# Moving 104 tiles of counting from layer 2 to layer 1 of a four-layer graph network, and placing the turned products later

## What is computed

```python
h = relu(layernorm(x)); x = x + concat(h, mean_over_edges(h[src])) @ W.T + b          # layer 0
h = relu(layernorm(x)); theta = h[dst] - h[src]                                        # layer 1
w = sigmoid(relu(theta @ W1 + b1) @ W2 + b2)
x = x + segment_sum(w * theta, dst) + indegree * (h @ W4 + b4)
h = relu(layernorm(x)); x = x + (h + l2norm(elu(mean(relu(h@Wp.T+bp)[src]) @ Wl.T + bl + h@Wr.T)))  # layer 2
h = relu(layernorm(x)); x = x + segment_sum((h @ Wrel[type])[src] * norm, dst) + h @ Wloop          # layer 3
```

## Time and profile before

| | us |
|---|---|
| median of 3 runs | 6365.12 (6364.78 to 6367.93) |
| the profiled execution, its span from first to last instruction | 6426.8 |
| layer 0, edges | 107.8 to 1240 |
| layer 1, edges | 1304.2 to 3660 |
| layer 2, edges | 3696 to 4315 |
| layer 3, edges | 4526 to 6426.8 |

### The profile page before, as it was taken

One profiled execution on the slowest core, in us unless ns is written; L12 is line 12 of the kernel. 1 busy time (PEld: TensorE's weight loads), 2 busy tenths in 40 slices (PEclk: granted clock), 3 DMA queues, 4 the chain that ended last, 5 costly groups with the idle time before them and its releaser, 6 DMA issues.

```text
span 6426.8 us, 68888 instructions
## 1 busy us (share of the span) xinstructions
PE 3872.2 (60%) x20122; PEld 2959.4 (46%) x20154; DVE 2933.5 (46%) x9989; ACT 1413.8 (22%) x5474; POOL 3972.3 (62%) x4198
## 2 busy tenths in 40 slices
PE   4676766655555565555555578876565565665433
PEld 3333434445544454455455456653344444444332
DVE  7555544556555565556555633342333222222222
ACT  4222122333333333333333401121000000000000
POOL 4556666456666666666666466646566666666665
PEclk7778778777777777777777789998777777777666
DMA  3333333345455454544545455555211111111121
GB/s 107 96 101 110 111 105 116 107 140 155 143 150 148 147 150 144 154 145 141 159 144 151 123 184 198 195 181 178 69 46 46 45 47 45 46 45 46 46 61 46
DMA packets 323521, 734.49 MB, mean 114 GB/s; under 512 B 77056, under 2 KB 164124, under 8 KB 310860
## 3 DMA queue, kind: packets, MB, share of 16 engines
q0 software_dynamic: 172432, 405.32, 23.2%
q1 hardware_dynamic: 148700, 323.81, 14.9%
q10 hardware_dynamic: 2016, 0.92, 0.1%
HBM read 598.71 MB, written 131.05 MB: 114 GB/s over the span
## 4 chain that ended last, share of the span: by engine, by line
another core or an unknown queue 30%; PE 27%; DVE 19%; issue 15%; ACT 4%; DMA 2%; DVEq 1%; SPq 1%; ACTq 0%
PE ps L2574 8%; DVE oneh L1863 6%; PE ps L2559 3%; PE ps L2530 3%; PE ps L2537 2%; DVE ps L1998 2%; PE ps L2469 2%; PE ps L2597 2%; DMA third<-dst_flat 2%; ACT turned_words L1681 1%; DVE third L1990 1%; PE ps L2419 1%; DVE turned_words L1955 1%; DVE tmp L1954 1%
## 5 line engine op out<-in xcount | busy, mean ns | idle before, releaser
L1470 POOL DMA_INDIRECT rows<-tab_rel,third x1299 | 1247.0, 960 | 646.9 <-issue 367.1
L1470 POOL DMA_INDIRECT rows<-tab_h,idx_src x1086 | 1046.7, 964 | 723.4 <-issue 345.8
L1470 POOL DMA_INDIRECT rows<-tab_hp,idx_src x1120 | 1077.1, 962 | 622.5 <-issue 298.8
L2597 PE MATMUL ps<-third 128*128 128x128 f32 x3126 | 607.1, 353 | 501.6 <-issue 295.8
L2530 PE MATMUL ps<-oneh,rows 128*128 128x128 f32 x2598 | 489.1, 340 | 607.1 <-DVE oneh L1863 330.7
L2597 PEld LDWEIGHTS ps<-third 128*128 128x128 f32 x3126 | 539.6, 258 | 593.7 <-issue 355.3
L2574 PE MATMUL ps<-third,h 128*120 128x384 bf16 (+17 forms) x3773 | 715.0, 337 | 65.8 <-issue 34.6
L2530 PEld LDWEIGHTS ps<-oneh,rows 128*128 128x128 f32 x2598 | 432.6, 245 | 695.8 <-DVE oneh L1863 362.6
L1681 ACT ACTIVATE turned_words<-turned_words 128x128 f32<-128x128 f32 x1563 | 463.1, 300 | 690.8 <-DVE turned_words L2003 527.5
L2574 PEld LDWEIGHTS ps<-third,h 128*120 128x120 bf16 (+10 forms) x3773 | 487.8, 133 | 239.4 <-issue 61.3
L1470 POOL DMA_INDIRECT third<-tab_hp,idx_src x443 | 425.9, 961 | 231.7 <-issue 118.5
(11 more groups left out here) (279 smaller groups left out, 5495.4 us busy)
## 6 DMA issues: line engine op xcount, KB each, us to landing
third<-dst_flat SPq DMA_DIRECT2D x390, 256.0 KB
h<-cnt_d SPq DMA_DIRECT2D x48, 1568.0 KB
cnt_d<-h SPq DMA_DIRECT2D x29, 1568.0 KB
cnt_d<-third SPq DMA_DIRECT2D x19, 1568.0 KB
tab_rel<-third SPq DMA_DIRECT2D x49, 512.0 KB
rows<-tab_rel,third POOLq DMA_INDIRECT x1299
rows<-tab_hp,idx_src POOLq DMA_INDIRECT x1120
rows<-tab_h,idx_src POOLq DMA_INDIRECT x1086
```

The lines of the kernel that those rows point to most:

```text
L1470: pool.indirect_dma_start(out=to[:, t, 0:n], out_offset=None, in_=table[:, :], in_offset=bass.IndirectOffsetOnAxis(ap=idx[:, col:col + 1], ...
L2597: last = pe.matmul(ps_t[sl][:, t * P:(t + 1) * P], onehT[:, sl, t * P:(t + 1) * P], pwin[:, st["v"] % 2, :], start=True, stop=True)
```

## The change

The share of layer 0 goes from 880/1563 to 980/1563. Rounded to bundles, it counts 976 tiles where it counted 872, which is six bundles more (of 18, 18, 18, 18, 16 and 16 tiles), and gathers 587 tiles where it gathered 691, 26 groups fewer. Layer 1 makes 192 late counts where it made 296, and stores 13 bundles where it stored 19. In layer 0 alone, `pack_turn` stands five tiles behind `pack_out` where it stood one, and `pack_add` three behind `pack_turn` where it stood one. Layers 2 and 3 keep their work.

```diff
-FIRST_SHARE = 880 / 1563
+FIRST_SHARE = 980 / 1563
+LATE_TURN, LATE_ADD = 5, 3
@@ multiply(u)
                 plan.append(("pack_out", st))
-                yield 0.0
+                for _ in range(LATE_TURN if layer == 0 else 1):
+                    yield 0.0
                 st["added"] = n_added.get(u - 1, 0)
                 plan.append(("pack_turn", st))
-                yield 0.0
+                for _ in range(LATE_ADD if layer == 0 else 1):
+                    yield 0.0
                 plan.append(("pack_add", dict(u=u, sums=sums, turn=n_turn[u], add=s_add.value)))
```

## The result

The changed kernel takes 6287.20 us (median of 4 runs, 6283.21 to 6294.15), the kernel before 6366.52 on the same chip (6364.78 to 6371.44). The ratio is 0.9879, with a 95% interval of 0.9862 to 0.9896: 79 us less, where 65 more were forecast.

A forecast was written before the change was run, and what follows sets the result against it. It took PE to bound layer 0, with gathers as unused cover. Terms +165 - 42 - 25 - 30 = +68 us on the 6365.12 us median gave 6433, said as 6430; range 6400 to 6475, 8 in 10 within 6360 to 6490.

The forecast's parts named there:

- the one on the gathers: Layer 0: gathers run ahead while POOL waits for PE, so fewer of them are worth nothing.
- Six bundles, +165: Layer 0: six added bundles at 27.5 us each, priced from PE's work, cost 165 us (138 to 180).
- 26 groups, -42: Layer 0: 26 fewer groups at 1.6 us each, mainly PE's scatters and turned sums, save 42 us (35 to 57).
- The later turn, -25: Layer 0: counts fill half of the 1.4 us hole before each of 35 turns, saving 25 us (0 to 50).
- Layer 1, -30: Layer 1: 104 fewer late counts save 5 us and six fewer stores 25, together 30 us (0 to 90).
- The turn's idle time: Rival, layer 0: PE's 193.8 us idle before turns is a real hole the later turn closes; 6264 us, chance 0.07.
- The clock: Rival, layer 0: PE's granted clock rises from 0.78 to 0.86, giving back 97 us; 6336 us, chance 0.08.
- HAM oscillation: Skill's rule on PE's clock: idle gaps halve the array's rate, so the later turn would be worth more than its hole.
- sign of being wrong: Layer 0 growing by less than 50 us (the clock or the turn), or layer 1 shrinking by more than 90.

The follow-up runs named there:

- e13: Against the kernel before: POOL fetches two of a group's four tiles in layer 0, 345 indirect DMAs fewer; ratio 0.9502.
- e7: Against the kernel before: DVE makes only the first and last of a group's four one-hot matrices in layer 0; ratio 0.9994.
- long sets: Sets of runs in which the kernel before took 6404, 6369 or 6359 us (first, fourth, fifth), and the timing of the change.
- e2: Against the kernel before: share 980/1563 only, turn and addition left one tile behind; 6329.14 us, ratio 0.9893.
- e16: Against the kernel before: share 1080/1563, turn five tiles and addition three tiles late; ratio 0.9722.
- e1: Against the kernel before: share kept at 880/1563, only turn five tiles and addition three tiles late; ratio 1.0015.
- short sets: Sets of runs in which the kernel before took 5476 us (second and third).
- e15: Against the kernel before: each bundle's table in layer 0 multiplied with 25 of 49 node blocks, 696 matmuls fewer; ratio 0.9972.
- set 1: First set of follow-up runs, trying the parts of the change separately; the kernel before took 6403.77 us in it.
- e3: Against the kernel before: share kept at 880/1563, turn five tiles late, addition one tile behind it; ratio 1.0031.
- e4: Against the kernel before: share kept at 880/1563, turn where it was, addition three tiles behind it; ratio 0.9991.
- set 4: Fourth set of follow-up runs, on gathers, products and other shares; the kernel before took 6369.00 us in it.
- e14: Against the kernel before: share 945/1563, turn five tiles and addition three tiles late; ratio 0.9888.
- e10: Against the kernel before, in the third set: share 980/1563 only, turn and addition one tile behind; ratio 0.9948.
- e12: Against the kernel before, in the third set: share 1080/1563, turn and addition one tile behind; ratio 1.0077.
- e11: The changed kernel itself against the kernel before, in the third set; ratio 0.9909.
- e17: Against the kernel before: share 1030/1563, turn five tiles and addition three tiles late; ratio 0.9831.

## Why the prediction was wrong

**The step that failed** is the one on the gathers: "The gathers themselves are worth nothing there, since POOL waits for PE; they are the cover that is not used." It was read from POOL's wait of 172.4 us for PE, and from the absence of any wait of PE for a row. The first is true and does not show the bound: e13 has 373.0 us of that wait with half of the gathers, and is 317.5 us faster. The second was read from a trace that lacks most of the events that would show it: for the 691 gathers of layer 0, which signal 16 times each, it holds 2544 landing events out of 11056, where e7's holds 10981 and lists 31.8 us of PE waiting for rows, 28 times. With a gather at 0.92 us (e13), 104 fewer are worth 96 us, not nothing.

What is shown in the long sets is that cost. By which way a gather costs it there, through POOL's own pace (1.25 us each is 864 us of layer 0's 1126.5) or through what gathers do to the moment at which PE's signals come (last section), is not: taking gathers away takes away both.

**Six bundles, +165.** With the 96 us known, the six bundles are what is missing to the measured change of layer 0. Layer 0 of the kernel before, then of e2:

```profile
107.80:1234.30 1126.50, 746.49 (x3565) 422.41 (x3565) 611.90 (x2704) 259.59 (x634) 667.94 (x691) 0.76 0.35 103
```

```profile
105.60:1158.30 1052.70, 802.44 (x3953) 456.66 (x3954) 642.11 (x2815) 301.85 (x738) 570.61 (x587) 0.81 0.35 110
```

1052.7 - 1126.5 is -74 = -96 + 22, so 3.7 us a bundle. From share 880 to 1080, e16 gives 984 - 1126 = -142 = -184 + 42 for twelve bundles: 3.5 each, or 1.8 against e1 (1146.4 us), whose turn is as late as e16's. All are remainders: no run adds bundles and keeps the gathers, and if a gather is worth more than 0.92, so is a bundle. I had taken 27.5. The price was not far off as a price of PE (19.5 in the short sets, and 23 for PE never kept waiting in the prediction). It was wrong to put it on the path: e15 takes 24 products out of each bundle and gains 0.6 us a bundle. Whether DVE's pairs or ACT's evictions bound a part of the layer in the long sets was not tried; e7, the one run with less work for DVE, was in a short set.

**26 groups, -42.** This is the same error from the other side: 1.6 us a group was PE's part (measured 1.4). With four gathers at 0.92 the group is worth about 3.7 us, and the term is -96 in place of -42. (The prediction has a group at 1.37 us in one place and 1.34 in another; nothing hangs on it.)

**The later turn, -25.** The hole of 1.4 us was sized rightly (1.38 in the short sets), and the reason for not gaining it, DVE's pairs, was named; it takes back all of it in the long sets (+9 us in e1) and half or more in the short ones.

**Layer 1, -30.** The changed kernel's layer 1 takes 2288.2 us from first to last gather (1245.0 to 3533.2), against 2338.0 before. Within a set the difference is smaller. In set 1 the three kernels with all 296 late counts take 2324.1, 2333.1 and 2327.8 us (e1, e3, e4), and e2 with 192 takes 2315.2. In set 4 e13 and e15 with 296 take 2308.5 and 2308.9, e14 with 224 takes 2285.2, and e16 with 96 takes 2280.0. So the term is -9 to -50 by single profiles, and its size was about right. In the short sets 296, 192 and 96 late counts give 1990.7, 1990.5 and 1985.0 us (e7, e10, e12): next to nothing. Whether the stores or the counts make the rest was not tried.

**The rivals.** The measured 6287 lies between what two of them gave, 6264 and 6336, and neither mechanism made it. The turn's idle time was not real, as said there. The clock did rise in layer 0, from 0.76 to 0.80, but not to the 0.84 from which that rival was to decide, and PE's products have next to no price there (e15), so it is a companion and not the cause: the clock rises where gathers, and with them PE's waits, get fewer (0.90 in e13) and falls to 0.71 in e15, where PE has less to do. By the rule that the prediction cites ("HAM oscillation" in the Trainium skill, TensorE: Matmul & The Clock Gate) the later turn would warm the array. The traces do not show it: e10 and e11 differ only in where the turn and the addition stand, and both have 0.89 in layer 0; the kernel before has 0.76 and e1 0.74. The holes that it closed were of 1.4 us. The prediction's own sign of being wrong, layer 0 growing by less than 50 us, came true, but it named the clock or the turn for it. That gathers pace the layer was not among my rivals at all.

**What could have told it beforehand.** Turns 36.8 us apart with 24 gathers between them are 1.53 us a gather, and layer 1, with entirely other work beside the gathers, goes at 1.498. Two stretches with one pace for each gather are a sign of a common bound. I used the second number only to show that late counts are free. It is a hint and no proof: in the long sets layer 0 takes 1.79 us a gather in e2, 2.00 in e16 and 2.30 in e13. In the short sets, where e7 has 1.33 in layer 0 and 1.27 in layer 1, it is plain.

## What to carry to other kernels

An engine that waits for a slot now and then can still set the pace: in e7 POOL waits 41.1 us for PE, and its gathers are the bound. Before an engine's work is called cover, compare time per unit of its work between stretches with different company; if it is the same, that engine or what it drags along is the first suspect, and a run with less of that work decides. Before an absent wait is taken as proof, look whether the trace has the events that would show it. And a price worked out from an engine's busy time is a price on the path only if something there shows that the engine is the path: here 19.5 us of PE work cost 2 to 4 in the long sets.

## What the runs showed of the hardware

The two kinds of set differ in when PE's signals come. In the short sets they come with PE's records; in the long ones they trail them while gathers are issued. The timeline of the kernel before (long) at a bundle's end:

```profile
1053.20 0.82 PE L2537 MATMUL ps<-rows,oneh 128*128 128x385 bf16 x4
...
1054.93 0.42 PE L2559 MATMUL ps<-turned_words,tmp 128*128 128x504 bf16 x2 [0.66 <-issue]
...
1062.45 0.95 POOL L1470 DMA_INDIRECT rows<-tab_h,idx_src  x1 [0.30 <-issue]
1065.79 0.58 ACT L1632 CAST h<-ps 128x504 bf16<-128x504 f32 x1 [11.05 <-remote]
1065.99 0.94 POOL L1470 DMA_INDIRECT rows<-tab_h,idx_src  x1 [2.59 <-remote]
```

PE has nothing new to record after 1055 until its turn at 1067.4, ACT gets its count at 1065.8, and POOL its slot at 1066.0; the event that frees it, of the scatter's semaphore, comes at 1065.73, where the last scatter was recorded at 1053.20. Counted from the trace's semaphore events, this is the share of PE's signals in layer 0 that come within 0.45 us of the start of their matmul's record:

| kernel | gathers in layer 0 | set | within 0.45 us |
|---|---|---|---|
| before | 691 | long | 0.49 |
| e15, half the products | 691 | long | 0.49 |
| changed | 587 | long | 0.59 |
| e17 | 539 | long | 0.64 |
| e16 | 491 | long | 0.78 |
| e13, half the gathers | 346 | long | 0.86 |
| e7 | 691 | short | 0.95 |
| e11, changed | 587 | short | 0.97 |

So the lateness goes with the gathers and not with PE's work, and it is there only in the long sets; it is a correlation in the traces, with e13 and e15 as the only interventions.

A signal without an event in the trace counts as late in this table, and the long sets have such. Between the first and the last gather of layer 0 the trace of the kernel before holds 1067 events for 1254 signals of PE, but also only 910 for 1300 of DVE and 431 for 621 of ACT; e7's holds 1265 for 1266, 1310 for 1311 and 627 for 628. Between the last gather of layer 0 and the first of layer 1, where nothing is gathered, the kernel before has every one. So in the long sets many waits have no releaser that could be found, which is part of what stands as "issue" and "remote" in its rows. The gathered data is as early as in the short sets: from the start of POOL's record to the last packet of its gather's data the median is 2.35 us in layer 0 of the kernel before, and 2.34 in e7.

In layer 1 of the long sets, where gathers never stop, one signal in ten comes so promptly (0.11 in the kernel before, 0.97 in e7), and the gaps between signals crowd at multiples of some 0.71 us (0.7, 1.4, 2.15, 2.85, 4.3 and 5.7 among them), where those of e7 gather at 0.8 and 1.7 us alone. POOL's own records, 0.94 us each and 1.25 from start to start, are the same in both. What holds PE's results back, and why a set is long or short on one and the same chip, stays open; the kernel's gain of 1.2% (long) and 0.9% (short) does not hang on it, but the way in which a gather costs 0.92 us in the long sets does.
